# Taking the low part of x on GpSimd instead of VectorE in a fused gated-attention and feed-forward kernel

## The chip, the cores and the metric

The kernel runs on one core of one Trainium2 chip. The metric is the device time of one execution in microseconds (us). Before the change three runs took 2694.0, 2697.14 and 2699.29 us; the median is 2697.14 us.

## What is computed

Two layers, each followed by a residual and a layer norm, on x of shape (8, 2048, 512) in float32. Cut to what matters:

```
rkv = x @ W_rkv + b_rkv;  r, k, v = split(rkv, 3)
r = sigmoid(r);  k = exp(k);  kv = k * v
u1, u2 = running sums along the sequence of kv and of k, decayed by lam per step
a = (u1 + gamma * kv) / (u2 + gamma * k + 1e-06) * r
z = layernorm(x + a @ W_o + b_o)
z_prev = z of the token before (zero for the first one)
xr, xk = mu_r * z + (1 - mu_r) * z_prev,  mu_k * z + (1 - mu_k) * z_prev
out = layernorm(z + sigmoid(xr @ W_r.T) * (relu(xk @ W_k.T) ** 2 @ W_v.T))
```

Every matrix product is formed from split operands. A float32 value f becomes a high part hi (f rounded to the type `float32r` that TensorE takes) and a low part lo = f - hi, and a product of two matrices is three matmuls: hi·hi, hi·lo and lo·hi.

## The kernel before, in words

The 16384 tokens are cut into 32 blocks of 512 tokens, four to a sequence. A step s (the functions called `step`, one for each engine) works on three blocks at once: the attention of block s, the output projection and most of the feed-forward layer of block s-1 (`s1`), and the last half of the feed-forward layer of block s-2 (`s2`). Each engine has its own list of instructions in the order in which the code issues them, and engines wait for one another on semaphores alone. The first three steps are written out; seven batches of four steps are the body of a loop on the chip (`steps`, lines 220 to 230); the last step, `last_block` and `last_half` follow.

A step of TensorE (lines 865 to 890) is: `project` of chunk 0 (k, v, r of 128 channels, 12 matmuls each, lines 787 to 789), `values` of the second half of s2 (called V below, lines 804 to 806), `attention_out` of s1, `project` of chunk 1 with `transposes`, `project` of chunk 2, `transposes`, `receptance` and `keys` of the first half of s1, `project` of chunk 3, then `values` of the first half, `receptance` and `keys` of the second half of s1. The projections of the next block come right behind. They need x_hi and x_lo of that block, four pieces of 128 channels by 512 tokens.

A block's x is prepared late in the step before: SyncE loads x_f (line 272) when the last projection has read x, ScalarE rounds it to x_hi (`x_high`, line 415), and VectorE subtracts (`x_low`, line 607). x_lo lies in the same memory as x_f. The first projection of the block waits for each piece of x_lo (line 785).

The work around the change, late in a step, in each engine's own order:

- VectorE: `denominator(s, 3)` (lines 633 to 651, ending with the reciprocal), `gated_values(s1, 0)` (line 710), **`x_low` of the next block (line 607)**, `numerator(s, 3)` (a scan on line 659, a copy of one column on line 662, a multiply-add on line 664), `statistics` of the first half of s1's output (lines 671 to 677), `key_low(s1, 1)` (line 702), which makes the low part of the operand of V.
- GpSimd: `mixed_low(s1, 1)` (line 341, two instructions), `residual(s1, 0)` (line 347, two; each waits for one of gated_values), `att(s, 3)` (line 316, which waits for the numerator and the reciprocal), `att_low(s, 3)` (line 320, which waits for ScalarE's high part, line 447), `inverse_std(s1, 1, 0)` (lines 325 to 334, which ends with `shift`), `bias_rows` (line 353, four).
- ScalarE: `x_high`, `att_high(s, 3)` (line 447), `normalise(s1, 1, 0)` (line 470, which waits for `shift`), `tanh(s1, 1)` (line 495), `key_square(s1, 1)` (lines 505 to 509), whose result `key_low(s1, 1)` waits for.

So ScalarE's tanh and key_square stand behind a normalise that waits for GpSimd, and V on TensorE in the next step waits for what VectorE makes of key_square.

Of the kernel before, what the change touches and what calls it, by code (L numbers as in the profile page):

```python
# [24 lines left out]
ALU = mybir.AluOpType  # L25
# [4 lines left out]
NC = H // P  # L30
# [40 lines left out]
def wait(eng, sem, value):  # L71
    if value is not None:
        eng.wait_ge(sem, value)
# [13 lines left out]
def program(nc, xT, x, w_rkv, w_o, w_r, w_k, w_v, b_rkv, b_o, nu_log, gamma_log, mu_r, mu_k, out, seq):  # L87
# [9 lines left out]
    with ExitStack() as ctx:  # L97
# [6 lines left out]
        def split(name, shape):  # L104

            hi = sb(name + "_hi", shape, F32R)
            value = sb(name + "_f", shape, F32)
            size = 4 * math.prod(shape[1:])
            lo = nc.alloc_sbuf_tensor_at(name + "_lo", shape, F32R, offset=nc.sbuf_base - size)
            return hi, lo, value  # L110
# [8 lines left out]
        x_hi, x_lo, x_f = split("x", [P, NC, TB])  # L119
# [61 lines left out]
        x_hi_made, x_lo_made = sem("x_hi_made"), sem("x_lo_made")  # L181
# [114 lines left out]
        @block.gpsimd  # L296
        def _(pool):
            pool.memset(zT[:, :, 0:1], 0.0).then_inc(s_col0, 1)
            pool.memset(zero[:], 0.0).then_inc(s_const, 1)
            pool.memset(half_pow[:], -0.5).then_inc(s_const, 1)  # L300
            pool.memset(eps_ln[:], EPS_LN).then_inc(s_const, 1)
            pool.memset(ident[:], 0.0).then_inc(s_id, 1)
            pool.wait_ge(s_id, 1)
            pool.affine_select(out=ident[:], in_=ident[:], compare_op=ALU.not_equal, fill=1.0,
                               base=0, pattern=[[-1, P]], channel_multiplier=1).then_inc(s_id, 1)
            pool.wait_ge(s_bo, 16)

            def weight_low(i):
                hi, lo, value, _ = w_rest[i]
                pool.wait_ge(w_hi_made, i + 1)  # L310
                pool.tensor_tensor(lo, value, hi, ALU.subtract).then_inc(w_lo_made, 1)

            def att(s, c):
                wait(pool, num_made, s.count(NC, c + 1))
                wait(pool, rec_made, s.count(NC, c + 1))
                pool.tensor_tensor(att_f[:, c], att_f[:, c], gate[:, c % 2], ALU.mult).then_inc(att_made, 1)  # L316

            def att_low(s, c):
                wait(pool, att_hi_made, s.count(NC, c + 1))
                pool.tensor_tensor(att_lo[:, c], att_f[:, c], att_hi[:, c], ALU.subtract).then_inc(att_lo_made, 1)  # L320

            def inverse_std(s, which, half):
                tiles = slice(HT * half, HT * half + HT)
                wait(pool, ln_mean[which], s.count(NT, HT * half + HT))
                pool.tensor_tensor(ve[:, which, tiles], mv[:, which, tiles, 1], eps_ln[:], ALU.add)\
                    .then_inc(ln_var[which], 1)
                pool.tensor_tensor(shift[:, which, tiles], zero[:, 0:HT, 0], mv[:, which, tiles, 0], ALU.subtract)\
                    .then_inc(ln_negated[which], 1)
                wait(pool, ln_var[which], s.count(NH, half + 1))
                pool.tensor_tensor(rstd[:, which, tiles], ve[:, which, tiles], half_pow[:], ALU.pow)\  # L330
                    .then_inc(ln_rstd[which], 1)
                wait(pool, ln_negated[which], s.count(NH, half + 1))
                wait(pool, ln_rstd[which], s.count(NH, half + 1))
                pool.tensor_tensor(shift[:, which, tiles], shift[:, which, tiles], rstd[:, which, tiles], ALU.mult)\  # L334
                    .then_inc(ln_shift[which], 1)

            def mixed_low(s, half, run):
                for lo, f, hi, hi_made, lo_made in r_and_k(run, (xr_lo, xr_f, xr_hi, xr_hi_made, xr_lo_made),
                                                           (xk_lo, xk_f, xk_hi, xk_hi_made, xk_lo_made)):
                    wait(pool, hi_made, s.count(NH, half + 1))  # L340
                    pool.tensor_tensor(lo[:], f[:], hi[:], ALU.subtract).then_inc(lo_made, 1)  # L341

            def residual(s, half):
                for i in range(HT):
                    tile = HT * half + i
                    wait(pool, o_made, s.count(NT, tile + 1))
                    pool.tensor_tensor(t[:, tile], t[:, tile], y[:, y_slot(s, tile)], ALU.add).then_inc(y2_made, 1)  # L347

            def bias_rows(s):
                for tile in (2, 3, 0, 1):  # L350
                    wait(pool, y_loaded[tile], s.count(16, 16))
                    rows = y[:, y_slot(s, tile)]
                    pool.tensor_tensor(rows, rows, bo[:], ALU.add).then_inc(y_biased, 1)

            def step(s):
                s1, s2 = s.back(1), s.back(2)
                first = s.batch is None and s.s == 0
                if s2.exists():
                    residual(s2, 1)
                if s1.exists():  # L360
                    inverse_std(s1, 0, 0)
                if s2.exists():
                    inverse_std(s2, 1, 1)
                if s1.exists():
                    inverse_std(s1, 0, 1)
                att(s, 0)
                att_low(s, 0)
                if first:
                    weight_low(W_WO)
                if s1.exists():  # L370
                    mixed_low(s1, 0, s)
                att(s, 1)
                att_low(s, 1)
                if first:
                    weight_low(W_R)
                att(s, 2)
                att_low(s, 2)
                if first:
                    weight_low(W_K)
                if s1.exists():  # L380
                    mixed_low(s1, 1, s)
                    residual(s1, 0)
                att(s, 3)
                att_low(s, 3)
                if first:
                    weight_low(W_V)
                if s1.exists():
                    inverse_std(s1, 1, 0)
                bias_rows(s)

            def last_block(s):
                s1, s2 = s.back(1), s.back(2)
                inverse_std(s1, 0, 0)
                residual(s2, 1)
                inverse_std(s1, 0, 1)
                inverse_std(s2, 1, 1)
                mixed_low(s1, 0, s)
                mixed_low(s1, 1, s)
                residual(s1, 0)
                inverse_std(s1, 1, 0)  # L400

            def last_half(s):
                residual(s.back(2), 1)
                inverse_std(s.back(2), 1, 1)

            steps(pool, step, last_block, last_half)
# [191 lines left out]
        def _(dve):  # L598
# [5 lines left out]
            def x_low(s):  # L604
                for c in range(NC):
                    wait(dve, x_hi_made, s.count(NC, c + 1))
                    dve.tensor_tensor(x_lo[:, c], x_f[:, c], x_hi[:, c], ALU.subtract).then_inc(x_lo_made, 1)  # L607
# [108 lines left out]
            def step(s):  # L716
                s1, s2 = s.back(1), s.back(2)
                first = s.batch is None and s.s == 0
                denominator(s, 0)
                if s2.exists():  # L720
                    gated_values(s2, 1)
                if s1.exists():
                    attention_rows(s1, 0)
                if s2.exists():
                    statistics(s2, 1, 1, result_rows(s2), y2_made)
                if s1.exists():
                    attention_rows(s1, 1)
                numerator(s, 0)
                if s1.exists():
                    mix(s1, 0, s)  # L730
                denominator(s, 1)
                numerator(s, 1)
                denominator(s, 2)
                numerator(s, 2)
                if s1.exists():
                    key_low(s1, 0)
                    mix(s1, 1, s)
                if first:
                    x_low(s.back(-1))
                denominator(s, 3)  # L740
                if s1.exists():
                    gated_values(s1, 0)
                if s.back(-1).exists() and not first:
                    x_low(s.back(-1))
                numerator(s, 3)
                if s1.exists():
                    statistics(s1, 1, 0, result_rows(s1), y2_made)
                    key_low(s1, 1)
# [207 lines left out]
```

## Time and profile before

| | |
|---|---|
| median of three runs | 2697.14 us |
| the profiled execution's own time | 2699.09 us |
| its span, from the first to the last instruction | 2697.3 us |
| granted TensorE clock, mean | 0.987 |
| TensorE matmul busy | 2560.1 us (95%) |
| VectorE busy | 2045.1 us (76%) |
| ScalarE busy | 1287.5 us (48%) |
| GpSimd busy | 1293.9 us (48%) |

In the profile PE is TensorE, DVE VectorE, ACT ScalarE, POOL GpSimd and SPq SyncE's queue of DMA issues. A row names the line of the code, the operation and its tiles (out<-in), how often it ran, and its time. Matmuls are pipelined and overlap in the records: one of 512 columns is shown with 0.39 us, and the next starts 0.23 us after it.

### The profile page before, as it was taken

To read this page: it belongs to the slowest core of one execution; us is meant where nothing else is said; L and a number is where in the kernel's file an instruction comes from. 1 tells how busy PE (TensorE), PEld (TensorE's weight loads), DVE (VectorE), ACT (ScalarE), POOL (GpSimd) and SP (SyncE) were. 2 spreads that over 40 slices of the span, in tenths; PEclk is the share of its full clock that TensorE was granted. 3 is DMA by queue.
4 is the path that set the end of the run, shared out by engine and by line. 5 is a ranking of instruction groups with operands and counts; after the bars stand their busy time and mean duration, and the time that the engine had idled before them with its cause. 6 is when DMAs were issued, how large, how long until landed. Compare 5 with 4: busy or idle time off the path is not lost.

```text
span 2697.3 us, 36409 instructions
## 1 busy us (share of the span) xinstructions
PE 2560.1 (95%) x12800; PEld 2166.3 (80%) x12800; DVE 2045.1 (76%) x2826; ACT 1287.5 (48%) x2255; POOL 1293.9 (48%) x1166
## 2 busy tenths in 40 slices
PE   7899999999999999999999999999999999999997
PEld 5788888878888888888888888888888888888886
DVE  8877778777778777877777777777877777777773
ACT  4445454544454444545454544445454444545454
POOL 3545454454554454454544544545445454454453
PEclk8999999999999999999999999999999999999998
DMA  4001111011010011110111100111101111101010
GB/s 168 16 32 48 32 48 40 24 48 48 32 48 32 33 47 36 44 40 27 46 48 32 48 32 32 47 32 48 40 24 47 48 33 40 39 32 47 32 32 24
DMA packets 57800, 110.89 MB, mean 41 GB/s; under 512 B 7040, under 2 KB 7040, under 8 KB 57088
## 3 DMA queue, kind: packets, MB, share of 16 engines
q1 hardware_dynamic: 57600, 108.31, 12.1%
q8 instruction: 115, 1.88, 0.3%
q14 instruction: 85, 0.70, 0.1%
HBM read 74.73 MB, written 33.55 MB: 40 GB/s over the span
## 4 chain that ended last, share of the span: by engine, by line
PE 47%; DVE 20%; ACT 13%; issue 12%; POOL 7%; DMA 1%; SPq 0%; DVEq 0%; ACTq 0%; POOLq 0%
PE bankB L804 8%; PE bankB L806 7%; PE bankB L805 7%; PE bankA L787 5%; PE bankA L789 5%; PE bankA L788 5%; DVE gate L648 4%; DVE x_lo L607 4%; POOL att_f L316 4%; PE bankB L852 3%; PE bankB L853 3%; PE bankB L854 3%; DVE att_f L659 3%; ACT t L470 2%; ACT xr_f L463 2%
## 5 line engine op out<-in xcount | busy, mean ns | idle before, releaser
L787 PE MATMUL bankA<-x_hi,wrkv_hi 128*128 128x512 f32 x1536 | 606.7, 395 | 26.2 <-DVE x_lo L607 11.4
L788 PE MATMUL bankA<-x_lo,wrkv_hi 128*128 128x512 f32 x1536 | 602.5, 392 | 0.0
L789 PE MATMUL bankA<-x_hi,wrkv_lo 128*128 128x512 f32 x1536 | 601.9, 392 | 0.0
L651 DVE RECIPROCAL gate<-gate 128x512 f32<-128x512 f32 x128 | 429.2, 3353 | 4.4
L316 POOL TENSOR_TENSOR att_f<-att_f,gate 128x512 f32<-128x512 f32 x128 | 205.2, 1603 | 381.5 <-DVE att_f L664 380.7
L320 POOL TENSOR_TENSOR att_lo<-att_f,att_hi 128x512 fp32r<-128x512 f32 x128 | 205.8, 1608 | 358.2 <-ACT att_hi L447 358.2
L787 PEld LDWEIGHTS bankA<-x_hi,wrkv_hi 128*128 128x128 f32 x1536 | 291.1, 190 | 87.8 <-issue 23.1
L852 PE MATMUL bankB<-xk_hi,wk_hi 128*128 128x256 f32 x1024 | 297.4, 290 | 64.7 <-ACT zT L455 58.9
L702 DVE TENSOR_TENSOR ka_lo<-ka_f,ka_hi 128x512 fp32r<-128x512 f32 x128 | 104.6, 817 | 334.4 <-ACT ka_f L509 334.4
L789 PEld LDWEIGHTS bankA<-x_hi,wrkv_lo 128*128 128x128 f32 x1536 | 290.8, 189 | 61.6
L347 POOL TENSOR_TENSOR t<-t,y 128x512 f32<-128x512 f32 x128 | 191.2, 1514 | 304.3 <-DVE t L710 304.3
L788 PEld LDWEIGHTS bankA<-x_lo,wrkv_hi 128*128 128x128 f32 x1536 | 291.1, 190 | 57.1
L447 ACT ACTIVATE att_hi<-att_f 128x512 fp32r<-128x512 f32 x128 | 80.1, 626 | 474.3 <-POOL att_f L316 474.3
L470 ACT ACTIVATE y<-y,shift,rstd 128x512 f32<-128x512 f32 x128 | 97.2, 810 | 436.8 <-POOL shift L334 436.7
L853 PE MATMUL bankB<-xk_lo,wk_hi 128*128 128x256 f32 x1024 | 294.0, 287 | 0.0
L854 PE MATMUL bankB<-xk_hi,wk_lo 128*128 128x256 f32 x1024 | 293.7, 287 | 0.0
L852 PEld LDWEIGHTS bankB<-xk_hi,wk_hi 128*128 128x128 f32 x1024 | 200.4, 196 | 79.8 <-ACT zT L455 76.3
L804 PE MATMUL bankB<-wv_hi,ka_hi 128*128 128x512 f32 x512 | 201.4, 393 | 19.3 <-DVE ka_lo L702 18.5
L341 POOL TENSOR_TENSOR xr_lo<-xr_f,xr_hi 128x1024 fp32r<-128x1024 f32 x64 | 166.6, 2603 | 110.3 <-ACT xr_hi L483 110.0
L804 PE MATMUL bankB<-wo_hi,att_hi 128*128 128x512 f32 x512 | 201.1, 393 | 11.9 <-POOL att_lo L320 9.9
L804 PE MATMUL bankB<-wr_hi,xr_hi 128*128 128x512 f32 x512 | 202.0, 395 | 0.0
L853 PEld LDWEIGHTS bankB<-xk_lo,wk_hi 128*128 128x128 f32 x1024 | 200.9, 196 | 1.2
(88 smaller groups left out, 5720.3 us busy)
## 6 DMA issues: line engine op xcount, KB each, us to landing
x_f<-in_xT SPq DMA_DIRECT2D x128, 256.0 KB, 4.0
y<-in_x SPq DMA_DIRECT2D x128, 256.0 KB, 2.7
out<-t SPq DMA_DIRECT2D x128, 256.0 KB, 2.0
wrkv_f<-in_w_rkv SPq DMA_DIRECT2D x3, 768.0 KB, 6.3
wo_f<-in_w_o SPq DMA_DIRECT2D x1, 1024.0 KB, 9.7
wr_f<-in_w_r SPq DMA_DIRECT2D x1, 1024.0 KB, 11.6
wk_f<-in_w_k SPq DMA_DIRECT2D x1, 1024.0 KB, 13.6
wv_f<-in_w_v SPq DMA_DIRECT2D x1, 1024.0 KB, 15.6
```

What stands on the lines that cost most here:

```text
L316: pool.tensor_tensor(att_f[:, c], att_f[:, c], gate[:, c % 2], ALU.mult).then_inc(att_made, 1)
L320: pool.tensor_tensor(att_lo[:, c], att_f[:, c], att_hi[:, c], ALU.subtract).then_inc(att_lo_made, 1)
L347: pool.tensor_tensor(t[:, tile], t[:, tile], y[:, y_slot(s, tile)], ALU.add).then_inc(y2_made, 1)
L651: dve.reciprocal(gate[:, c % 2], gate[:, c % 2]).then_inc(rec_made, 1)
L787: pe.matmul(bank[:], w_hi, x_hi[:, h], start=(h == 0), stop=False)
L788: pe.matmul(bank[:], w_hi, x_lo[:, h], start=False, stop=False)
L789: last = pe.matmul(bank[:], w_lo, x_hi[:, h], start=False, stop=(h == NC - 1))
L804: pe.matmul(bank[:], hi, w_hi[:, c], start=(c == 0), stop=False)
L805: pe.matmul(bank[:], hi, w_lo[:, c], start=False, stop=False)
L852: pe.matmul(dst, wk_hi[:, c, cols], xk_hi[:, c], start=(c == 0), stop=False)
L853: pe.matmul(dst, wk_hi[:, c, cols], xk_lo[:, c], start=False, stop=False)
L854: last = pe.matmul(dst, wk_lo[:, c, cols], xk_hi[:, c], start=False, stop=(c == NC - 1))
```

## The change

`x_low` of the next block goes from VectorE's list to GpSimd's. On VectorE it stood between `gated_values(s1, 0)` and `numerator(s, 3)`; on GpSimd it stands between `att(s, 3)` and `att_low(s, 3)`. The subtraction, its operands, the semaphore it waits for and the one it raises are the same. In the first step, and ahead of the steps, x_low stays on VectorE, so of the 32 blocks 30 change the engine.

```diff
@@ GpSimd
+            def x_low(s):
+                for c in range(NC):
+                    wait(pool, x_hi_made, s.count(NC, c + 1))
+                    pool.tensor_tensor(x_lo[:, c], x_f[:, c], x_hi[:, c], ALU.subtract).then_inc(x_lo_made, 1)
+
...
                 att(s, 3)
+                if s.back(-1).exists() and not first:
+                    x_low(s.back(-1))
                 att_low(s, 3)
@@ VectorE
                 denominator(s, 3)
                 if s1.exists():
                     gated_values(s1, 0)
-                if s.back(-1).exists() and not first:
-                    x_low(s.back(-1))
                 numerator(s, 3)
```

VectorE's list before, in the third step, from the reciprocal of chunk 3 to the end of the statistics (t is gated_values, att_f the numerator, st and mv the statistics):

```order
L651 RECIPROCAL gate<-gate 128x512
L710 SCALAR_TENSOR_TENSOR t<-t,bankB 128x512 x2
L607 TENSOR_TENSOR x_lo<-x_f,x_hi 128x512 x4
L659 SCALAR_TENSOR_TENSOR att_f<-lam,carry,kv 128x512
L662 COPY carry<-att_f 128x1
L664 SCALAR_TENSOR_TENSOR att_f<-kv,gamma,att_f 128x512
L671 BN_STATS st<-t 128x6 x2
```

The same stretch of VectorE's list in the changed kernel (line numbers behind the new function are 5 to 7 higher):

```order
L658 RECIPROCAL gate<-gate 128x512
L717 SCALAR_TENSOR_TENSOR t<-t,bankB 128x512 x2
L666 SCALAR_TENSOR_TENSOR att_f<-lam,carry,kv 128x512
L669 COPY carry<-att_f 128x1
L671 SCALAR_TENSOR_TENSOR att_f<-kv,gamma,att_f 128x512
L678 BN_STATS st<-t 128x6 x2
```

The four subtractions are gone, and the numerator follows on gated_values. GpSimd's list before, in the same step, from the low parts of the mixed rows to the bias (the second t is residual, ve to shift are inverse_std, y is bias_rows):

```order
L341 TENSOR_TENSOR xr_lo<-xr_f,xr_hi 128x1024
L341 TENSOR_TENSOR xk_lo<-xk_f,xk_hi 128x1024
L347 TENSOR_TENSOR t<-t,y 128x512 x2
L316 TENSOR_TENSOR att_f<-att_f,gate 128x512
L320 TENSOR_TENSOR att_lo<-att_f,att_hi 128x512
L325 TENSOR_TENSOR ve<-mv,eps_ln 128x2
L327 TENSOR_TENSOR shift<-zero,mv 128x2
```

And in the changed kernel:

```order
L341 TENSOR_TENSOR xr_lo<-xr_f,xr_hi 128x1024
L341 TENSOR_TENSOR xk_lo<-xk_f,xk_hi 128x1024
L347 TENSOR_TENSOR t<-t,y 128x512 x2
L316 TENSOR_TENSOR att_f<-att_f,gate 128x512
L352 TENSOR_TENSOR x_lo<-x_f,x_hi 128x512 x4
L320 TENSOR_TENSOR att_lo<-att_f,att_hi 128x512
L325 TENSOR_TENSOR ve<-mv,eps_ln 128x2
L327 TENSOR_TENSOR shift<-zero,mv 128x2
```

The four subtractions now stand ahead of att_low and of inverse_std in GpSimd's list. ScalarE's, TensorE's and SyncE's lists are as before.

## Rows read from the trace of the kernel before

**Rows 1.** The page, busy time, share of the span and instructions of each engine.

```profile
PE 2560.1 (95%) x12800; PEld 2166.3 (80%) x12800; DVE 2045.1 (76%) x2826; ACT 1287.5 (48%) x2255; POOL 1293.9 (48%) x1166
```

**Rows 2.** Waits of the whole span: who waited for whom, us in total, times, longest.

```profile
ACT t L470 <- POOL shift L334: 92.4, 33, 7.9
...
PE bankB L852 <- ACT zT L455: 58.9, 31, 2.1
...
PE bankB L804 <- DVE ka_lo L702: 18.5, 23, 0.8
...
PE bankA L787 <- issue: 9.9, 6, 1.9
```

**Rows 3.** Timeline of TensorE, late in step 15 and into 16: start, us, instruction, [idle before].

```profile
1295.76 0.40 PE L787 MATMUL bankA<-x_hi,wrkv_hi 128*128 128x512 f32 x1
...
1304.93 0.47 PE L804 MATMUL bankB<-wv_hi,ka_hi 128*128 128x512 f32 x1 [0.83 <-DVE ka_lo L702]
```

**Rows 4.** Timeline of VectorE, the same stretch (neighbours of one kind merged).

```profile
1284.79 1.22 DVE L710 SCALAR_TENSOR_TENSOR t<-t,bankB 128x512 f32<-128x512 f32 x2
1285.92 5.12 DVE L607 TENSOR_TENSOR x_lo<-x_f,x_hi 128x512 fp32r<-128x512 f32 x4
1290.96 1.27 DVE L659 TENSOR_TENSOR_SCAN att_f<-lam,carry,kv 128x512 f32<-128x512 f32 x1
...
1292.46 0.75 DVE L664 SCALAR_TENSOR_TENSOR att_f<-kv,gamma,att_f 128x512 f32<-128x512 f32 x1
...
1302.28 1.19 DVE L702 TENSOR_TENSOR ka_lo<-ka_f,ka_hi 128x512 fp32r<-128x512 f32 x1 [7.59 <-ACT ka_f L509]
1304.10 0.69 DVE L702 TENSOR_TENSOR ka_lo<-ka_f,ka_hi 128x512 fp32r<-128x512 f32 x1 [0.63 <-ACT ka_f L509]
```

**Rows 5.** Timeline of GpSimd, the same stretch.

```profile
1284.07 2.42 POOL L341 TENSOR_TENSOR xk_lo<-xk_f,xk_hi 128x1024 fp32r<-128x1024 f32 x1
1286.43 3.46 POOL L347 TENSOR_TENSOR t<-t,y 128x512 f32<-128x512 f32 x2
1293.29 1.29 POOL L316 TENSOR_TENSOR att_f<-att_f,gate 128x512 f32<-128x512 f32 x1 [3.40 <-DVE att_f L664]
1295.33 1.29 POOL L320 TENSOR_TENSOR att_lo<-att_f,att_hi 128x512 fp32r<-128x512 f32 x1 [0.74 <-ACT att_hi L447]
...
1297.72 0.20 POOL L334 TENSOR_TENSOR shift<-shift,rstd 128x2 f32<-128x2 f32 x1
1297.87 5.05 POOL L353 TENSOR_TENSOR y<-y,bo 128x512 f32<-128x512 f32 x4
```

**Rows 6.** Timeline of ScalarE, the same stretch.

```profile
1297.95 1.52 ACT L470 ACTIVATE t<-t,shift,rstd 128x512 f32<-128x512 f32 x2 [2.70 <-POOL shift L334]
```

**Rows 7.** Timeline of VectorE, middle of step 16: instructions beside busy GpSimd.

```profile
1332.41 1.22 DVE L633 TENSOR_TENSOR_SCAN u<-lam,key 128x512 f32<-128x512 f32 x1
...
1335.31 2.77 DVE L648 SCALAR_TENSOR_TENSOR gate<-key,gate 128x512 f32<-128x512 f32 x1
...
1359.25 1.85 DVE L633 TENSOR_TENSOR_SCAN u<-lam,key 128x512 f32<-128x512 f32 x1 [0.43 <-ACT key L434]
```

**Rows 8.** Timeline of GpSimd, step 16: what ran at those times, and an undisturbed pair.

```profile
1312.09 2.54 POOL L347 TENSOR_TENSOR t<-t,y 128x512 f32<-128x512 f32 x2 [9.18 <-DVE t L710]
...
1332.58 2.15 POOL L320 TENSOR_TENSOR att_lo<-att_f,att_hi 128x512 fp32r<-128x512 f32 x1 [5.24 <-ACT att_hi L447]
1334.76 2.77 POOL L341 TENSOR_TENSOR xr_lo<-xr_f,xr_hi 128x1024 fp32r<-128x1024 f32 x1
...
1358.72 1.29 POOL L320 TENSOR_TENSOR att_lo<-att_f,att_hi 128x512 fp32r<-128x512 f32 x1 [4.52 <-ACT att_hi L447]
```

**Rows 9.** Stretches: busy us (instructions) of PE, PEld, DVE, ACT, POOL; granted clock; DMA.

```profile
1264.50:1267.90 3.40, 3.40 (x18) 3.40 (x17) 3.40 (x2) 0.51 (x2) 0.33 (x1) 0.50 0.00 0
...
2257.80:2261.20 3.40, 3.40 (x18) 3.40 (x17) 3.40 (x2) 0.94 (x2) 0.74 (x1) 0.50 0.00 0
2261.20:2264.60 3.40, 3.40 (x30) 3.40 (x30) 2.25 (x4) 1.86 (x3) 1.30 (x1) 1.00 0.00 0
```

## The prediction, made before the changed kernel ran

> **What bounds the kernel now.** I read the shares of busy time first: TensorE is at 95% [rows 1], so a change elsewhere pays or costs only through the pauses that it shortens or lengthens there. The table of waits names them [rows 2]. One before keys (L852) comes once a step and lasts 1.9 us (58.9 over 31); it waits for ScalarE's zT and lies ahead of the change. One before V (L804) waits for ka_lo in 23 steps, 0.80 us each. In six other steps, where the loop on the chip turns over, TensorE pauses for "issue" instead, 1.65 us each (9.9 over 6), and V then waits for nothing.
>
> The pause before V is the one that the change can reach, so I followed it back in the timelines of one step; the steps repeat within a tenth of a microsecond or two. V starts at 1304.93, 0.83 us late [rows 3], right behind the second ka_lo, which ends at 1304.79 [rows 4]. VectorE had been idle for 7.59 us before ka_lo, so ScalarE was late, not VectorE. ScalarE stood at normalise until 1297.95, waiting for shift [rows 6], with tanh and key_square queued behind. shift ends GpSimd's list att, att_low, inverse_std [rows 5], and att waited 3.40 us for the numerator, which on VectorE stood behind x_low [rows 4]. So x_low is on the path: x_lo, numerator, att, att_hi, att_low, shift, normalise, key_square, ka_lo, V. The reader should see that shift matters, not VectorE's load: after the statistics VectorE idles anyway.
>
> **What the change removes.** x_lo held VectorE from 1285.92 to the scan's start at 1290.96, 5.04 us [rows 4]. Now the scan can be issued at 1285.92.
>
> **What it adds.** Four subtractions of 128x512 in GpSimd's list between att and att_low. The nearest row is bias_rows, the same size and also two inputs, 5.05 us for four back to back, 1.26 each [rows 5]. I take 5.0 us from start to start. att_low and inverse_std, and with them shift, come behind it.
>
> [...]
>
> **How early att can start.** It waits for the numerator and, in its own list, for the two residuals. Two-input instructions of VectorE and GpSimd hold each other up in this trace. A scan issued at 1359.25 took 1.85 us and ended 1.09 us after the att_low that was running ended at 1360.01 [rows 7, 8]. An att_low issued just behind a scan took 2.15 us instead of 1.29 and ended 1.10 us after the scan. A multiply-add issued behind xr_lo took 2.77 us and ended 0.55 us after it [rows 7, 8]. The two residuals take 3.46 us beside x_lo [rows 5] and 2.54 us elsewhere [rows 8]. Replaying the place with these values: xk_lo ends at 1286.49 [rows 5]; the scan, already waiting, ends 1.08 later at 1287.57; residual 1 ends 1.1 later at 1288.7; the multiply-add, issued at about 1287.8 behind the copy, ends 0.57 later at 1289.25; residual 2 ends 1.1 later at 1290.35; then att, with the numerator long ready. att starts at 1290.3 and not at 1293.29: 3.0 us earlier.
>
> **The sum for one step.** att from 1290.3, x_low from 1291.6, att_low from 1296.6 (att_hi, made in the meantime, no longer holds it up), shift done at 1299.15, since it ends 2.59 us after att_low's start [rows 5]. Before, it was 1297.92. So shift is 1.25 us later: 5.0 for x_low, less 3.0 for the earlier att, less the 0.74 us of waiting for att_hi [rows 5]. normalise, tanh, key_square, ka_lo and V follow shift one for one. bias_rows moves along too, so its overlap with the first ka_lo stays. Bounds: with no mutual hold-up the residuals end at 1289.0 and shift at 1297.85, 0.07 us earlier than now; with every GpSimd instruction of this stretch at the 1.73 us of a residual beside x_lo (half of 3.46) instead of 1.26, shift is 3 us later.
>
> **The sum for the kernel.** 30 blocks change the engine. In 24 steps (the 23 of the row and one that the view books elsewhere) V's pause grows by all of 1.25 us: 30.0 us. In the six loop steps V has 1.65 - 0.80 = 0.85 us in hand, and 0.40 remains: 2.4 us. TensorE runs through from V to the projections of chunk 1, on which the rest of the step hangs, so nothing later gives this back. Sum 32 us.
>
> **The clock.** V's pause becomes 0.80 + 1.25 = 2.05 us, as long as the longest before keys (2.1) [rows 2]. After such pauses the granted clock fell six times between 100 and 2600 us, from 1.00 to 0.50 (1.2 GHz) for 3.4 us at a time; the first and the last of the six are shown [rows 9]. Four followed a keys pause of a loop step, two a loop pause. In such a stretch 18 matmuls of 256 columns start where the next has 30, so a fall costs 12 starts of 0.12 us, about 1.5 us. Of the six loop steps' long keys pauses four were followed by a fall; of all 37 pauses, six. I take half of the 24 new ones: 12 x 1.5 = 18 us; bounds 0 and 24 x 1.5 = 36 us.
>
> Total 32 + 18 = 50 us on the profiled execution's 2699.1, so 2749; that execution lay 2 us above the median, so 2747.
>
> **Costed at nothing.** VectorE's gain of 5 us: it waits for ka_f there anyway; if it didn't, the gain would be the pause, 0.8 us a step. x_lo's readiness: its pieces end at about 1292.9, 1294.1, 1295.4 and 1296.6, while TensorE wants the first at 1295.76 [rows 3] and the fourth nine matmuls of 0.23 us later, 1297.8. 1.2 us remain. If that is used up, V's longer pause absorbs it first. att_low's delay: attention_out comes behind V, over 13 us later. SyncE's list is passed by nothing.
>
> **Rivals.**
> - *Not slower.* The residuals run beside the numerator unhindered. Then shift comes at 1297.85, V's pause stays 0.8 us, and the time is 2699.1 - 2 - 0.07 x 24, about 2695. It decides this way if att starts by 1289.1. For it: the residuals beside VectorE's work on y take 2.54 us [rows 8]. Against: all the pairs of rows 7 and 8. 8%.
> - *Faster.* shift comes 0.8 us earlier and V's pause goes: 2697 - 19 = 2678. GpSimd's list alone, from xk_lo's end at 1286.49, holds 2.5 + 1.26 + 5.0 + 1.26 + 1.3 = 11.3 us and ends at 1297.8, so this needs subtractions below 1.1 us, and no row of that size shows that. 3%.
> - *Much slower.* GpSimd's stretch runs at the disturbed 1.73 us. shift comes 3 us later; x_lo's last piece is about 1 us too late, inside V's pause. 24 x 3 + 6 x 2.15 = 85, with 18 for the clock: 2800. Against: VectorE does one-input statistics there, beside which att takes 1.29 us [rows 5]. 7%.
> - *It does not do what it says*: the two lists above show that it does; only the first two blocks stay on VectorE.
>
> **How the numbers follow.** My case has the other 82%: 1.0 to 1.6 us a step, with 0 to 24 falls. 24 x 1.0 + 6 x 0.15 = 25 without a fall gives 2722; 24 x 1.6 + 6 x 0.75 = 43 with 24 falls gives 2776. For 8 in 10 I take 2714 to 2772, which leaves out most of the rivals and the ends. About 0.2%, 5.4 us, can be told from no change. Slower by more: my case and the much slower one, 0.89; the same 0.08; faster 0.03.
>
> **What would show it.** Right: x_lo on GpSimd at 1.25 us a piece; att about 3 us earlier against gated_values, shift 1.2 later; residuals still near 3.7 us for two; the wait of L804 for ka_lo at some 2 us, 24 times; more stretches at 0.50. Wrong: that wait at 0.8 us or gone, or TensorE waiting for x_lo in each step, or a clock that never falls after V's pause (then 2729).

## The result, and the profile after

The changed kernel takes 2758.56 us (median of four runs, 2756.04 to 2761.68) against 2698.22 us for the kernel before, measured beside it: a ratio of 1.0225, with a 95% interval of 1.0206 to 1.0244. It is 60 us slower; 50 had been forecast, with 2747 us as the time. The profiled execution took 2756.04 us, its span is 2754.2 us.

The page of the changed kernel, the row that answers to [rows 1]:

```profile
PE 2582.3 (94%) x12800; PEld 2186.6 (79%) x12800; DVE 1930.0 (70%) x2706; ACT 1287.3 (47%) x2255; POOL 1447.9 (53%) x1286
```

VectorE lost 115 us of work and GpSimd gained 154. The end of the program follows neither. The waits of the changed kernel, as in [rows 2] (line numbers are up to 7 higher):

```profile
ACT t L477 <- POOL shift L334: 219.1, 33, 7.9
...
PE bankB L857 <- ACT zT L462: 59.2, 31, 2.1
PE bankB L809 <- DVE ka_lo L709: 48.1, 25, 2.1
```

ScalarE's wait for shift grew from 92.4 to 219.1 us. Only a part of that is lateness: in one step it went from 2.70 us [rows 6] to 6.92, of which 1.24 us are the later shift; the rest is that ScalarE is through with att_high 3 us sooner, because att is, and then waits longer.

```profile
1331.83 1.52 ACT L477 ACTIVATE t<-t,shift,rstd 128x512 f32<-128x512 f32 x2 [6.92 <-POOL shift L334]
```

TensorE's wait for ka_lo ahead of V went from 18.5 to 48.1 us; the pause ahead of keys stayed, 59.2 against 58.9. How one step got there, on GpSimd, to be held against [rows 5]:

```profile
1316.72 2.42 POOL L341 TENSOR_TENSOR xk_lo<-xk_f,xk_hi 128x1024 fp32r<-128x1024 f32 x1
1319.09 3.91 POOL L347 TENSOR_TENSOR t<-t,y 128x512 f32<-128x512 f32 x2
1322.96 1.28 POOL L316 TENSOR_TENSOR att_f<-att_f,gate 128x512 f32<-128x512 f32 x1
1324.20 5.05 POOL L352 TENSOR_TENSOR x_lo<-x_f,x_hi 128x512 fp32r<-128x512 f32 x4
1329.21 1.29 POOL L320 TENSOR_TENSOR att_lo<-att_f,att_hi 128x512 fp32r<-128x512 f32 x1
...
1331.60 0.20 POOL L334 TENSOR_TENSOR shift<-shift,rstd 128x2 f32<-128x2 f32 x1
```

And on VectorE in the same stretch, to be held against [rows 4]:

```profile
1317.43 1.22 DVE L717 SCALAR_TENSOR_TENSOR t<-t,bankB 128x512 f32<-128x512 f32 x2
1318.56 1.65 DVE L666 TENSOR_TENSOR_SCAN att_f<-lam,carry,kv 128x512 f32<-128x512 f32 x1
...
1320.44 1.41 DVE L671 SCALAR_TENSOR_TENSOR att_f<-kv,gamma,att_f 128x512 f32<-128x512 f32 x1
...
1336.17 1.18 DVE L709 TENSOR_TENSOR ka_lo<-ka_f,ka_hi 128x512 fp32r<-128x512 f32 x1 [12.16 <-ACT ka_f L516]
1337.98 0.69 DVE L709 TENSOR_TENSOR ka_lo<-ka_f,ka_hi 128x512 fp32r<-128x512 f32 x1 [0.63 <-ACT ka_f L516]
```

Count from the end of gated_values, 1317.43 + 1.22 = 1318.65 here and 1286.01 before. att started 7.28 us behind it before and starts 4.31 us behind it now. shift ended 11.91 us behind it and ends 13.15 us behind it now: 1.24 us later. VectorE's own work is done by 1324, and it then stands idle for 12.16 us instead of 7.59. V on TensorE, against [rows 3]:

```profile
1338.82 0.47 PE L809 MATMUL bankB<-wv_hi,ka_hi 128*128 128x512 f32 x1 [2.07 <-DVE ka_lo L709]
```

The longer pauses come to about 31 us (48.1 + 2.0 booked under "issue", less 18.5 + 0.8). The span grew by 57 us, so some 26 us are elsewhere. Most of them are in the clock. Between 100 and 2600 us the granted clock fell from 1.00 to 0.50 twenty times, for 3.4 us each, and before it fell six times; in the whole span it fell 28 and 13 times. The traces give the clock as a share only. In the fall at 1264.5 us of the kernel before [rows 9] the matmuls of 256 columns start 0.213 us apart (10 starts from 1264.98 to 1267.11 us), and 0.12 us apart behind it. 256 columns in 0.213 us are 1.2 a nanosecond. The prediction's 1.2 GHz is this number read as one column a clock, an estimate of mine; its 1.5 us for a fall does not use it. What a fall costs can be read from whole steps, each taken from its first keys product to that of the next step. First two starts of the kernel before, with no fall between them, then three of the changed kernel, with no fall between the first two and one between the last two:

```profile
1098.79 0.39 PE L852 MATMUL bankB<-xk_hi,wk_hi 128*128 128x256 f32 x1 [1.97 <-ACT zT L455]
1180.76 0.38 PE L852 MATMUL bankB<-xk_hi,wk_hi 128*128 128x256 f32 x1 [1.96 <-ACT zT L455]
```

```profile
1380.83 0.39 PE L857 MATMUL bankB<-xk_hi,wk_hi 128*128 128x256 f32 x1 [1.85 <-ACT zT L462]
1464.02 0.39 PE L857 MATMUL bankB<-xk_hi,wk_hi 128*128 128x256 f32 x1 [1.96 <-ACT zT L462]
1548.68 0.39 PE L857 MATMUL bankB<-xk_hi,wk_hi 128*128 128x256 f32 x1 [1.95 <-ACT zT L462]
```

The three steps take 81.97, 83.19 and 84.66 us. So a plain step, one in which the loop on the chip does not turn over, got about 1.2 us longer, and a fall costs about 1.5 us. In the whole span the longer steps make 32 us (24 plain steps, and six loop steps that grew by 0.3) and 15 more falls 22 us. Another 2.4 us lie ahead of the first keys product, which starts at 116.74 instead of 114.36 us. No x_low is on GpSimd so early, and that start varies without the change: 116.48 us in run 9 and 113.80 in run 10 below.

One stretch of a fall in the changed kernel and the stretch behind it, the columns as in [rows 9]:

```profile
1044.90:1048.30 3.40, 3.40 (x18) 3.40 (x18) 3.37 (x3) 0.23 (x2) 0.00 (x0) 0.50 0.00 0
1048.30:1051.70 3.40, 3.40 (x27) 3.28 (x27) 1.74 (x3) 2.31 (x4) 1.29 (x1) 1.00 0.02 5
```

This fall comes behind a keys pause, and so do 16 of the 20; three come behind loop pauses (those where the loop turns over) and one behind V's. That was not forecast: the keys pause is as long as it was, and V's is the one that grew.

### The profile page after: what moved, and what is told of

Read it like the earlier page. It is cut to its first block, busy times and chain, and to the rows that moved or that the text cites. A ratio compares the mean times of both kernels' runs of the same rounds, so it can differ in the third digit from the quotient of the medians.

```text
span 2754.2 us, 36409 instructions
## 1 busy us (share of the span) xinstructions
PE 2582.3 (94%) x12800; PEld 2186.6 (79%) x12800; DVE 1930.0 (70%) x2706; ACT 1287.3 (47%) x2255; POOL 1447.9 (53%) x1286
## 3 DMA queue, kind: packets, MB, share of 16 engines
q1 hardware_dynamic: 57600, 108.31, 11.8%
## 4 chain that ended last, share of the span: by engine, by line
PE 42%; POOL 20%; DVE 13%; ACT 13%; issue 11%; DMA 1%; SPq 0%; ACTq 0%; POOLq 0%; DVEq 0%
PE bankB L809 7%; PE bankB L810 7%; PE bankB L811 7%; POOL x_lo L352 5%; PE bankA L792 5%; PE bankA L794 5%; PE bankA L793 5%; POOL att_f L316 4%; DVE gate L655 3%; POOL t L347 3%; PE bankB L857 3%; PE bankB L858 3%; PE bankB L859 3%; POOL xk_lo L341 2%; POOL xr_lo L341 2%
## 5 line engine op out<-in xcount | busy, mean ns | idle before, releaser
L857 PE MATMUL bankB<-xk_hi,wk_hi 128*128 128x256 f32 x1024 | 305.7, 299 | 65.0 <-ACT zT L462 59.2
L347 POOL TENSOR_TENSOR t<-t,y 128x512 f32<-128x512 f32 x128 | 205.1, 1622 | 304.7 <-DVE t L717 304.7
L858 PE MATMUL bankB<-xk_lo,wk_hi 128*128 128x256 f32 x1024 | 302.4, 295 | 0.0
L859 PE MATMUL bankB<-xk_hi,wk_lo 128*128 128x256 f32 x1024 | 302.0, 295 | 0.0
L857 PEld LDWEIGHTS bankB<-xk_hi,wk_hi 128*128 128x128 f32 x1024 | 209.0, 204 | 80.1 <-ACT zT L462 76.6
L809 PE MATMUL bankB<-wv_hi,ka_hi 128*128 128x512 f32 x512 | 203.1, 397 | 50.2 <-DVE ka_lo L709 48.1
L809 PE MATMUL bankB<-wo_hi,att_hi 128*128 128x512 f32 x512 | 201.3, 393 | 11.9 <-POOL att_lo L320 9.8
L858 PEld LDWEIGHTS bankB<-xk_lo,wk_hi 128*128 128x128 f32 x1024 | 209.3, 204 | 1.2
L859 PEld LDWEIGHTS bankB<-xk_hi,wk_lo 128*128 128x128 f32 x1024 | 209.4, 205 | 0.0
```

The lines of the kernel that those rows point to most:

```text
L809: pe.matmul(bank[:], hi, w_hi[:, c], start=(c == 0), stop=False)
L857: pe.matmul(dst, wk_hi[:, c, cols], xk_hi[:, c], start=(c == 0), stop=False)
L858: pe.matmul(dst, wk_hi[:, c, cols], xk_lo[:, c], start=False, stop=False)
L859: last = pe.matmul(dst, wk_lo[:, c, cols], xk_hi[:, c], start=False, stop=(c == NC - 1))
```

## The experiments

Three things are open behind the result. Is it really the order in which things reach shift that costs the 31 or 32 us? Do residual and numerator hold each other up as the replay had it? And what brings the falls of the clock? Falls are counted between 100 and 2600 us in the trace of one profiled execution of each kernel.

**1. x_low on VectorE, behind the numerator.**

```diff
                 if s1.exists():
                     gated_values(s1, 0)
-                if s.back(-1).exists() and not first:
-                    x_low(s.back(-1))
                 numerator(s, 3)
+                if s.back(-1).exists() and not first:
+                    x_low(s.back(-1))
```

> The kernel before, with x_low still on VectorE but issued behind numerator(s, 3) instead of ahead of it. Theory (the order ahead of shift decides, not the engine's load): att starts some 2 to 3 us earlier than before, shift at least 1.3 us earlier, V no longer waits for ka_lo, and 24 pauses of 0.8 to 1.0 us go: 2698 - 19 to 23 = about 2677, give or take 8 us for falls of the clock. Rival (x_low delays its followers wherever it stands, since it now competes with att and att_low on GpSimd): V's pause stays at 0.8 us, 2698. TensorE should not wait for x_lo by either.

Measured: 2697.13 us, ratio 0.9994 (0.9982 to 1.0005): no change, with 7 falls. The time was the rival's, but in the main not for its reason. VectorE's gated_values and GpSimd's timeline in this kernel:

```profile
1283.27 1.22 DVE L710 SCALAR_TENSOR_TENSOR t<-t,bankB 128x512 f32<-128x512 f32 x2
```

```profile
1288.80 1.74 POOL L316 TENSOR_TENSOR att_f<-att_f,gate 128x512 f32<-128x512 f32 x1
1291.29 1.56 POOL L320 TENSOR_TENSOR att_lo<-att_f,att_hi 128x512 fp32r<-128x512 f32 x1 [0.74 <-ACT att_hi L447]
1294.95 0.20 POOL L325 TENSOR_TENSOR ve<-mv,eps_ln 128x2 f32<-128x2 f32 x1 [2.11 <-DVE mv L677]
...
1296.10 0.19 POOL L334 TENSOR_TENSOR shift<-shift,rstd 128x2 f32<-128x2 f32 x1
```

att starts 4.3 us behind gated_values (which ends at 1284.49), 3 us earlier than in the kernel before. Then inverse_std waits 2.11 us for mv: the statistics, which I had left behind x_low on VectorE, now end last, and shift ends 11.8 us behind gated_values against 11.9 before. The competition that the rival named is there, att and att_low take 1.74 and 1.56 us instead of 1.29, but those 0.7 us go into the 2.11 us of waiting for mv. Two things feed shift, and moving one away from behind x_low leaves the other there.

**2. x_low on VectorE, behind the statistics.** The same edit, with x_low behind `statistics(s1, 1, 0)`.

> The kernel before, with x_low on VectorE behind statistics(s1, 1, 0) and ahead of key_low. In the run with x_low behind the numerator the statistics came 4 us late and took the numerator's place as what shift waits for, so shift stayed where it was. Theory (shift waits for the last of numerator and statistics on VectorE and of GpSimd's own list): now neither is behind x_low, shift ends some 2 us earlier against gated_values than before (11.9 us behind it before), V no longer waits for ka_lo, 24 x 0.8 to 0.97 = 19 to 23 us go, about 2677; the shorter step may bring other falls of the clock, up to 10 us more. Rival (x_low on VectorE holds up att and att_low on GpSimd wherever it stands): V's pause stays above 0.5 us and the time above 2690.

Measured: 2698.3 us against 2701.35, ratio 0.9987 (0.9977 to 0.9997). The waits of TensorE in this kernel, and its clock:

```profile
PE bankB L853 <- ACT zT L455: 59.1, 31, 2.1
PE bankA L788 <- DVE x_lo L607: 13.2, 2, 7.3
PE bankA L788 <- issue: 10.4, 6, 1.9
```

```profile
core 0: 2698.4 us, clock 0.976
```

The wait for ka_lo is gone, so that part of the theory held; shift ends 10.1 us behind gated_values, 1.8 us earlier than before:

```profile
1285.84 1.22 DVE L710 SCALAR_TENSOR_TENSOR t<-t,bankB 128x512 f32<-128x512 f32 x2
```

```profile
1296.97 0.20 POOL L334 TENSOR_TENSOR shift<-shift,rstd 128x2 f32<-128x2 f32 x1
```

A step without a fall takes 80.9 us, 1.05 less than before, which is 25 us in 24 steps; 3 us reach the end. The clock fell 23 times instead of six, 20 of them behind keys pauses and three behind loop pauses. 17 more falls at 1.5 us are another 25 us, where the expectation had 10 at most: the gain was given back there, as the next run shows.

**3. The same, with the keys pause filled.** Seven matmuls that nothing uses are issued ahead of the first keys product, into a bank that the next projection overwrites:

```diff
+            def useless(bank, n):
+                for _ in range(n):
+                    pe.matmul(bank[:], wrkv_hi[:, 0, 0, 0], x_hi[:, 0], start=True, stop=True)
...
+                    wait(pe, gate_exp, s.count(NC, 2))
+                    useless(bankA[1], 7)
                     keys(s1, 0, s)
```

> The same, with seven matmuls (1.59 us) that nothing uses in the pause ahead of the first keys product. If the falls of the clock come behind those pauses, they go: the number of falls between 100 and 2600 us drops to the two or three behind loop pauses, and the time is that of the run without them less 1.5 us for each fall that it had; with 6 to 12 falls there, 9 to 18 us less, about 2665. If falls are not tied to a pause, nothing changes.

Measured: 2667.34 us, ratio 0.9885 (0.9870 to 0.9899), faster than both kernels. No fall is left between 100 and 2600 us:

```profile
PE bankB L853 <- ACT zT L455: 11.5, 30, 0.5
```

```profile
core 0: 2661.3 us, clock 0.992
```

Seven matmuls without a use bring 31 us against run 2, some 1.35 us for each of the 23 falls; between the two profiled executions, in which the falls were counted, it is 37 us and 1.6. They cost nothing of their own: a step without a fall still takes 80.9 us. The 20 falls behind keys pauses are tied to TensorE's pause there, since they go when it is filled. The three behind loop pauses went as well, which the theory did not have: six loop pauses of up to 1.9 us are still there, with no fall behind them. Why is not shown.

**4. The changed kernel, with V's pause filled.** Six such matmuls ahead of V, in the plain steps.

```diff
                 if s2.exists():
+                    if s.batch is None or s.s >= 0:
+                        bank_free(s, "V", HT)
+                        useless(psum_of("V", HT), 6)
                     values(s2, 1, s)
```

> The changed kernel, with six matmuls of 512 columns whose result nothing uses issued in the pause ahead of V (not in the loop steps); they take 1.36 us of the 2.2 us, so the step is as long as in the changed kernel. Theory 1 (the clock falls because V's pause got long, as predicted): the falls go back from 21 to about 6, some 15 x 1.5 us less, about 2736. Theory 2 (the falls come behind the keys pauses, and only because the longer step moves the times at which these pauses come): 15 or more falls stay and the time stays within 6 us of 2758.

Measured: 2754.35 us, ratio 1.0219 (1.0202 to 1.0236), within 6 us of the changed kernel. The pause ahead of V is back to 0.7 us in the 23 steps that have the matmuls (the 2.0 of the row is in a step without them), and the falls stay: 19 between 100 and 2600 us, every one behind a keys pause.

```profile
PE bankB L809 <- DVE ka_lo L709: 18.6, 26, 2.0
```

```profile
core 0: 2752.0 us, clock 0.979
```

Theory 1, the one of the prediction, does not explain these falls.

**5. The changed kernel, with the keys pause filled** (the edit of run 3).

> The changed kernel, with seven such matmuls (1.59 us) issued in the pause ahead of the first keys product, the pause that the change did not touch. Theory 2: the 16 falls behind these pauses go, 16 x 1.5 = 24 us, about 2734, and V's pauses of 2.2 us stay with few falls behind them. Theory 1: falls stay behind V's pauses, about 2750 or more.

Measured: 2739.45 us, ratio 1.0166 (1.0149 to 1.0183), between what the theories gave. The falls behind the keys pauses go, but 10 come, all behind V's pauses of 2.1 us, where the changed kernel had one:

```profile
PE bankB L809 <- DVE ka_lo L709: 48.6, 27, 2.1
...
PE bankB L857 <- ACT zT L462: 11.7, 30, 0.5
```

So V's pause can bring a fall as well: ten here, and in run 10, with V's pause filled too, there are two falls in all. Theory 2 as I had put it is too narrow. That V's pauses do it here because they come at other times is my guess; this run does not show it.

**6. The kernel before, with a longer step.** Six such matmuls behind the wait for ka_lo and ahead of V, in the plain steps. TensorE is busy with them, and no pause grows.

```diff
                 if s2.exists():
+                    if s.batch is None or s.s >= 0:
+                        bank_free(s, "V", HT)
+                        wait(pe, ka_lo_made, s2.count(NT, 2 + 2))
+                        useless(psum_of("V", HT), 6)
                     values(s2, 1, s)
```

> The kernel before, with six such matmuls behind the wait for ka_lo and ahead of V in the plain steps: the step gets 1.36 us longer as in the changed kernel, but with TensorE busy, and no pause grows. Both theories: 23 x 1.36 = 31 us from the matmuls. Theory 1: the falls stay near 6, about 2730. Theory 2: the falls behind the keys pauses rise to 15 or so, another 13 us or more, about 2745 to 2752.

Measured: 2749.27 us, ratio 1.0198 (1.0181 to 1.0215). Its pauses are those of the kernel before, and its clock is that of the changed one:

```profile
PE bankB L852 <- ACT zT L455: 59.2, 31, 2.1
PE bankB L867 <- DVE ka_lo L702: 18.7, 23, 0.8
```

```profile
core 0: 2750.0 us, clock 0.978
```

The clock fell 20 times, 19 of them behind keys pauses. 31 us are the added matmuls, and the other 20 go with 14 more falls, about 1.4 us each. With pauses as long as before, in the same places of the step, a step that is 1.36 us longer was enough.

**7. x_low on GpSimd, behind shift.**

```diff
                 att(s, 3)
-                if s.back(-1).exists() and not first:
-                    x_low(s.back(-1))
                 att_low(s, 3)
...
                     inverse_std(s1, 1, 0)
+                if s.back(-1).exists() and not first:
+                    x_low(s.back(-1))
                 bias_rows(s)
```

> The changed kernel, with x_low on GpSimd behind inverse_std(s1, 1, 0) and ahead of bias_rows instead of between att and att_low. Theory (GpSimd's four subtractions of 1.25 us fit nowhere in its list late in the step): shift comes about 3 us earlier than before and V's pause goes, but the four pieces end at about 0.5, 1.0, 1.6 and 2.2 us too late for the projections, so TensorE waits for x_lo, 2.2 us a step in all, in place of 0.97 for ka_lo: 2698 + 24 x 1.2 + 6 x 0.5 = 2730, and up to 20 us more with falls. Rival (the change lost its time through the place in the list alone): below 2690.

Measured: 2752.22 us, ratio 1.0195 (1.0181 to 1.0210), with 21 falls. V's pause is gone, and TensorE waits for x_lo instead, in short pauses one piece after another:

```profile
PE bankA L792 <- POOL x_lo L352: 37.3, 102, 2.0
```

A step without a fall takes 83.1 us, 1.2 more than before, as the theory had it; the falls brought the time just above its 2730 to 2750. Neither of the two places tried in GpSimd's list has room for these 5 us: ahead of shift they delay V, behind it the next projections. Other places in that list were not tried.

**8. The changed kernel, with the residuals cut to one column.**

```diff
-                    pool.tensor_tensor(t[:, tile], t[:, tile], y[:, y_slot(s, tile)], ALU.add).then_inc(y2_made, 1)
+                    cols = slice(0, 1) if half == 0 else slice(0, H)
+                    pool.tensor_tensor(t[:, tile, cols], t[:, tile, cols], y[:, y_slot(s, tile), cols],
+                                       ALU.add).then_inc(y2_made, 1)
```

> The changed kernel, with residual(s1, 0) on GpSimd working on one column of 512, so the first half of each block's output leaves out the sum with z. Theory (residual and numerator hold each other up, so att starts 4.3 us behind gated_values): without the residuals the scan ends about 1.6 us and the multiply-add about 2.5 us behind gated_values, att starts about 2.5 us behind it, shift is 1.8 us earlier than in the changed kernel, and V's pause falls from 2.2 to about 0.4 us. Rival (no hold-up; the residuals only take their own time of 2.5 us): att starts at most 0.8 us earlier than in the changed kernel and V's pause stays at 1.4 us or more.

One execution took 2693.79 us, with 11 falls. This kernel leaves out the sum with z in the first half of each block, so the trace counts here and not the time. VectorE's timeline, then GpSimd's:

```profile
1283.04 1.22 DVE L719 SCALAR_TENSOR_TENSOR t<-t,bankB 128x512 f32<-128x512 f32 x2
...
1286.04 0.75 DVE L673 SCALAR_TENSOR_TENSOR att_f<-kv,gamma,att_f 128x512 f32<-128x512 f32 x1
```

```profile
1286.88 1.29 POOL L316 TENSOR_TENSOR att_f<-att_f,gate 128x512 f32<-128x512 f32 x1 [0.93 <-DVE att_f L673]
...
1295.52 0.20 POOL L334 TENSOR_TENSOR shift<-shift,rstd 128x2 f32<-128x2 f32 x1
```

att starts 2.62 us behind gated_values (1284.26) instead of 4.31, and the multiply-add takes 0.75 us instead of 1.41. V's pause is 8.8 us over 23 waits, 0.38 us each; the rival wanted 1.4 or more. shift ends 11.46 us behind gated_values instead of 13.15, 1.7 us earlier where 1.8 was expected. The hold-up is real, and it has the size of the replay.

**9 and 10. The change with the pauses filled on both sides.** To price shift apart from the clock: the kernel before with the keys pause filled (run 3's edit), and the changed kernel with both pauses filled (those of runs 3 and 4).

> The kernel before, with seven matmuls that nothing uses in the pause ahead of the first keys product. Theory: the four falls behind these pauses go and the two or so behind loop pauses stay: 2698 less 4 x 1.5 = 2692. If the seven matmuls cost something of their own, the time rises above 2698.

> The changed kernel with both pauses filled: seven such matmuls ahead of keys and six ahead of V. Theory (the change costs 32 us through shift, and the rest through falls of the clock): nearly all falls go, and the time is that of the before kernel with the filled keys pause plus 32, about 2724. Rival (more than shift is late on the path): it stays above 2735 with few falls.

Measured side by side: 2690.35 us, ratio 0.9981 (0.9970 to 0.9991), without a fall between 100 and 2600 us, and 2725.56 us, ratio 1.0108 (1.0089 to 1.0127), with two falls. Their clocks, before and after:

```profile
core 0: 2688.3 us, clock 0.991
```

```profile
core 0: 2722.7 us, clock 0.991
```

In the kernel before the two falls behind loop pauses, which were expected to stay, went too, as in run 3. At the same clock the change costs the difference of the ratios, 0.0127, 34 us, of which the two falls are about 3; this is the theory's 32, and the rival's 2735 us were not reached. The rest of the 0.0225 goes with the clock: some 26 us by the ratios, 22 by the spans of the profiled executions (57 less 34).

## Why the prediction was right, and where it was not

**The path** was read rightly. shift decides, not VectorE's load: VectorE lost 115 us of work and V came later; with x_low out of the way of both numerator and statistics (run 2), V's wait went.

**The replay of one step** held within a tenth of a microsecond. att was to start at 4.3 us behind gated_values and starts at 4.31; shift was to come 1.25 us later and comes 1.24 later; the four subtractions were to take 5.0 us from start to start and take 5.01; V's pause was to be 2.05 us and is 2.07. The rival without a hold-up falls by run 8. The hold-up shows in the changed kernel as well: 3.91 us for the two residuals beside the numerator, against 2.54 us for the undisturbed pair [rows 8].

One bound was worked out too low. With the residuals, att, the four subtractions and att_low at 1.73 us each from 1286.43, shift ends at 1301.6, 3.7 us later than before and not 3, so the much slower rival would have come out some 20 us higher. The pieces took 1.25 us, so nothing hung on it.

**The sum over the steps**, 32 us, is confirmed by the pauses (31 us), by the steps without a fall (81.97 and 83.19 us in the rows above) and by runs 9 and 10 (34 us with two falls in it).

**x_lo in time, and no faster case.** TensorE did not wait for x_lo in the plain steps. In three of the six loop steps its loop pause now ends with x_lo (4.4 us in all), but these pauses did not grow: 5.6 + 4.4 us against 9.9. Run 7 shows how near the limit is: behind shift, x_lo comes too late.

**The term that failed is the clock.** It had 12 falls behind V's longer pauses, 18 us. There are 14 more falls between 100 and 2600 us, about 21 us; but they came behind the keys pauses, which did not grow. That the numbers are near each other is luck. "V's pause becomes 2.05 us, as long as the longest before keys" was no reason for the number: with V's pause filled, 19 falls stay (run 4), and with no pause grown and only the step longer, 20 come (run 6). Where the keys pause was left as it was, the number of falls goes with the length of a step without a fall: 23 at 80.9 us (run 2), 11 at 81.5 (run 8), 7 and 6 at 81.8 and 81.9 (run 1 and the kernel before), and 19 to 21 at 83.1 to 83.3 (the changed kernel and runs 4, 6 and 7). I read this as the change moving the times at which pauses come that had long been there; no run moves these times alone, so that reading is not shown. The prediction had named a clock that never falls behind V's pause as a sign that it was wrong, with 2729 us then; it fell there once in the profiled execution, and yet the time was not 2729.

The price of a fall, 1.5 us from [rows 9], held: 1.4 to 1.5 us between steps with a fall and steps without one. The time lies 11 us over the forecast. On the profiled execution it is 7 (2756 against 2749): 22 instead of 18 us for the falls, and the 2.4 us ahead of the first keys product. The other 4.5 are that the forecast took the median to lie 2 us below the profiled execution, and it lies 2.5 above. The profiled one had the highest granted clock of the four, 0.978; the others had 0.975 to 0.977.

Why one of two equal pauses is followed by a fall and the other not is not settled by these runs. Six, 20 and 23 falls were seen with the same 31 keys pauses, in steps of three lengths. Chance alone does not pick them: in run 4 the falls come in a steady rhythm, about 167 and 85 us apart in turn, from 200 to 2473 us.

## What to carry to other kernels

Ask what the next waiting engine waits for, and follow every input of it: shift had the numerator, the statistics and GpSimd's own list, and the gain came only when none of the three was late. An engine that is half idle on average can be full at the place where work is put: GpSimd, busy for 53% of the span in the changed kernel, runs without a gap from 1314.35 to 1331.80 us. Replay that place instruction by instruction, with hold-ups from neighbouring rows. And where TensorE pauses for 2 us again and again, look at the granted clock before and after any change: here a step that got shorter by 1 us won 3 of 25 us until the remaining pause was filled.

## What the runs showed that I had not expected

A change that grows no pause can triple the falls of the clock: 6 before, 20 in run 6, with TensorE busy in every microsecond that was added; a step that got shorter brought 23. And work without a use can pay: seven matmuls of 512 columns a step, 1.59 us in a pause of 2 us, took 23 falls away and 31 us of time (2698.3 to 2667.34 us), at no cost that shows, and the result is the best kernel of this study.
